# Second layer of the expert network: blocks 1 to 23 by seven block products instead of eight, interleaved with the groups of the first layer; ScalarE centers rows

## The reference

```python
top_w, top_i = jax.lax.top_k(rw_tok, K)            # K = 2 experts, the same for all tokens
top_w = jax.nn.softmax(top_w, axis=-1)
h = jax.nn.gelu(jnp.einsum('nd,edf->enf', xf, W1) + b1[:, None, :], approximate=False)   # 256 -> 512
y = jnp.einsum('enf,efd->end', h, W2) + b2[:, None, :]                                   # 512 -> 256
out = jnp.einsum('ne,end->nd', w_dense, y)
out = _layer_norm(out + x, gamma, beta)            # the expert network's own x is normalised
x = x + out
```

## Time and profile before

| | us |
|---|---|
| median of 3 runs | 804.6 |
| profiled execution | 804.91 |
| its span | 803.0 |
| TensorE busy in the span | 761.0 |
| VectorE, ScalarE, GpSimd busy | 567.7, 479.4, 414.3 |
| TensorE busy in 500.96 to 782.78 us | 281.82 |

### The profile page before, as it was taken

One profiled execution on the slowest core, in us unless ns is written; L12 is line 12 of the kernel. 1 busy time (PEld: TensorE's weight loads), 2 busy tenths in 40 slices (PEclk: granted clock), 3 DMA queues, 4 the chain that ended last, 5 costly groups with the idle time before them and its releaser, 6 DMA issues. The chain is left out here.

```text
span 803.0 us, 15427 instructions
## 1 busy us (share of the span) xinstructions
PE 761.0 (95%) x4960; PEld 622.9 (78%) x4960; DVE 567.7 (71%) x1623; ACT 479.4 (60%) x1113; POOL 414.3 (52%) x649
## 2 busy tenths in 40 slices
PE   6899999999899999999849999999999999999996
PEld 5678888888566666676526788888888888888885
DVE  6863488788678888888888755655666666566656
ACT  2467345989899988888728425444444444444440
POOL 3430778778458888888717712333333333333323
PEclk9999999999999999999959989999999999999999
DMA  8855122222112211212101040000000000000001
GB/s 217 208 158 161 39 58 51 59 52 53 26 32 63 59 51 35 62 25 65 42 22 38 20 130 3 27 13 26 14 27 16 24 25 16 26 14 26 16 25 38
DMA packets 35423, 41.33 MB, mean 51 GB/s; under 512 B 11520, under 2 KB 20696, under 8 KB 35339
## 3 DMA queue, kind: packets, MB, share of 16 engines
q1 hardware_dynamic: 22355, 30.71, 13.3%
q0 software_dynamic: 8000, 6.82, 3.9%
q10 hardware_dynamic: 4984, 2.79, 1.5%
HBM read 25.59 MB, written 14.60 MB: 50 GB/s over the span
## 5 line engine op out<-in xcount | busy, mean ns | idle before, releaser
L1379 PE MATMUL ps<-Z 128*125 128x256 f32 x800 | 195.5, 379 | 0.7 <-DVE L L1987 0.7
L1379 PEld LDWEIGHTS ps<-Z 128*125 128x125 f32 x800 | 149.6, 187 | 22.2 <-DVE L L1987 1.1
L1116 PE MATMUL ps<-Z,L 128*128 128x250 f32 x600 | 126.9, 373 | 0.0
L1116 PEld LDWEIGHTS ps<-Z,L 128*128 128x128 f32 x600 | 113.6, 189 | 13.2
L1007 ACT ACTIVATE Z<-Z,b1s 128x250 f32<-128x250 f32 x144 | 68.4, 503 | 78.6 <-DVE Z L1980 78.5
L1980 DVE TENSOR_TENSOR Z<-ps,L 128x250 f32<-128x250 f32 x144 | 60.1, 419 | 76.8 <-PE ps L1362 76.6
L700 POOL TENSOR_SCALAR zr<-zmv 125x1 f32<-125x1 f32 x50 | 11.5, 230 | 199.3 <-issue 189.4
L1014 ACT ACTIVATE L<-ps 128x250 f32<-128x250 f32 x144 | 54.4, 380 | 65.5 <-PE ps L1362 63.6
L1236 PE MATMUL ps<-wr,Z 128*125 128x256 f32 x400 | 92.7, 384 | 0.0
L1362 PE MATMUL ps<-L 128*128 128x250 f32 x288 | 84.0, 374 | 0.0
L852 ACT ACTIVATE Z<-Z,bn_o,bn_s 128x250 f32<-128x250 f32 x150 | 81.2, 599 | 1.0 <-DVE bn_o L1690 1.0
...
## 6 DMA issues: line engine op xcount, KB each, us to landing
...
```

Of the source, the lines that this page charges most:

```text
L1116: last = mm(ps[:, group_bank(n), h * BT:(h + 1) * BT], wq[:, k, c * 128:(c + 1) * 128], h_raw(b, k), start=(k == 0), stop=(k == KD - 1))
L1379: last = mm(ps[0:TP, R_BANK + t, 0:D], ge_of(b, f)[:, t * TP:(t + 1) * TP], w2s[:, f // NF, f % NF, :], start=(k == 0), stop=(k == TOP_K * ...
```

## The change

For blocks 1 to 23 the second layer is computed by seven block products as well (`result_times`): the 250 x 1024 by 1024 x 256 product of a block is cut in two token halves, two experts and two output halves (`HD2` = 128 columns). Each product is four matmuls of 128 x 125 stationary by 128 x 128 moving. Blocks 0 and 24 keep the plain form (`whole_result`). With it come:

- four sums of GELU outputs for each block on GpSimd (`sum_of_g`, tensors of 128 x 500), and four sums of `w2s` once on VectorE (`weight_sum`);
- seven reads of PSUM by VectorE for each block, 125 x 128 each (`take_part`), in place of two of 125 x 256;
- rows centered by ScalarE (`center`), so that `make_row` on VectorE is one instruction;
- both halves' scale in one pair of GpSimd instructions (`z_scale`);
- the first layer's two blocks of a pair change places (`blocks`), so that the block consumed first has its GELU outputs first;
- other places for the tensors, and PSUM banks shared between slots: 0 and 1 for the first layer's sums, 2 and 3, 6 and 7 for the second layer.

```diff
+            def sum_of_g(b, i):
+                if i == S_1:
+                    pool.wait_ge(gelu_done, gelu_of_block(b))
+                after = {S_1: P5, S_2: P6, S_4: P3, S_3: P7}[i]
+                if b >= 2:
+                    pool.wait_ge(y_part.sem, y_part.count(b - 2, after))
+                if i == S_1:
+                    g.tensor_tensor(gs[:, 0], ge_part(b, 0, 1), ge_part(b, 1, 1), ALU.add).then_inc(n.sem, 1)
...
-            for s in range(SLOTS + 5):
-                n = s - 3
-                if n >= 0:
-                    z_scale(n)
-                if 0 <= n + 1 < TB * NB:
-                    x_and_offset(n + 1)
-                if s + NF < SLOTS:
-                    sum_of_h(s // NF + 1, s % NF)
+            for b in range(-1, NB - 1):
+                if b >= 1:
+                    for i in (S_1, S_2, S_4):
+                        sum_of_g(b, i)
+                    z_scale(b - 1)
+                    sum_of_g(b, S_3)
+                if b >= 0:
+                    x_and_offset(b)
+                p, half = divmod(b + 3, 2)
+                if NF * p < SLOTS:
+                    for i in range(2 * half, 2 * half + 2):
+                        sum_of_h(p, i)
...
+            def center(b, t):
...
+                a_.activation(za(b, t)[0:TP], x_of(b, t), ACT.Identity, bias=negmu[0:TP, b, t:t + 1]).then_inc(centered, 1)
...
+            center(0, 1)
+            center(0, 0)
             for i, l in ((1, 2), (2, 2), (1, 1), (2, 1)):
...
+            def result_times(b, n):
+                of = {P1: ge_part(b, 0, 0), P5: gs[:, 0], P6: gs[:, 1], P3: gs[:, 3],
+                      P7: gs[:, 2], P2: ge_part(b, 1, 0), P4: ge_part(b, 1, 1)}[n]
...
+                if n == P7:
+                    pe.wait_ge(g_sums.sem, g_sums.count(b - 1, S_3))
+                    pe.wait_ge(y_sum.sem, y_sum.count(b - 1, KEPT_U))
...
+                for k in range(NF):
+                    last = mm(ps[0:TP, bank, 0:HD2], of[:, k], by[:, k], start=(first and k == 0),
+                              stop=(k == NF - 1), skip_group_check=True)
+                last.then_inc(y_part.sem, 1)
+
+            def whole_result(b, t, k0, k1):
+                for k in range(k0, k1):
+                    f = F_ORDER[k]
+                    if k == 0 and t == 0:
+                        if b:
+                            pe.wait_ge(y_sum.sem, y_sum.count(b - 2))
...
+            for b in range(1, NB - 2):
+                g = 2 * b + 2
+                times(g, P1)
+                times(g, P5)
+                result_times(b, P1)
...
+            for n in (P1, P5, P6, P3, P7, P2, P4):
+                result_times(NB - 2, n)
+            for t in range(TB):
+                whole_result(NB - 1, t, 0, 8)
...
+            def take_part(b, n):
+                x_, z_, y_ = (ps[0:TP, bank, 0:HD2] for bank in (XR_BANK[b % 2], ZR_BANK, YR_BANK))
+                after, to, part, other, needs = {
+                    KEPT_1: (P1, kz[0][0:TP], x_, za(b, 0)[0:TP, lo], None),
+                    KEPT_5: (P5, kz[1][0:TP], z_, za(b, 1)[0:TP, hi], None),
+                    KEPT_U: (P6, kz[2][0:TP], x_, za(b, 0)[0:TP, hi], None),
+                    Z_12: (P3, zz[0][0:TP, hi], z_, kz[2][0:TP], KEPT_U),
+                    Z_22: (P7, zz[1][0:TP, hi], x_, kz[1][0:TP], KEPT_5),
+                    Z_11: (P2, zz[0][0:TP, lo], y_, kz[0][0:TP], KEPT_1),
+                    Z_21: (P4, zz[1][0:TP, lo], x_, za(b, 1)[0:TP, lo], None)}[n]
...
+                v_.tensor_tensor(to, part, other, ALU.add).then_inc(y_sum.sem, 1)
...
+                take_part(b, Z_12)
+                make_y(b - 1, 0)
+                sum_of_products(g + 1, SUM_12)
+                make_row(b + 1, 0)
+                take_part(b, Z_22)
+                sum_of_products(g + 1, SUM_22)
+                make_y(b - 1, 1)
+                sum_of_products(g + 1, SUM_11)
+                take_part(b, Z_11)
...
+            b = NB - 2
+            take_part(b - 1, Z_21)
+            stats(b - 1, 0)
+            take_part(b, KEPT_1)
...
+            make_y(b - 1, 1)
+            stats(b, 0)
+            take_part(b, Z_21)
+            stats(b, 1)
```

More of the change, by code:

```diff
@@ L444, in gps_layer @@
         SUM_12, SUM_22, SUM_11 = 1, 2, 3
+        S_1, S_2, S_4, S_3 = 1, 2, 3, 4
+        Z_12, Z_22, Z_11, Z_21 = 4, 5, 6, 7
+        STATS, MOMENTS = (1, 2), (3, 4)
         F_ORDER = (0, 2, 1, 3, 4, 6, 5, 7)
@@ L1972, in sum_of_products @@
                 f1, f2 = NF * e + c, NF * e + c + 2
+                b1_, b2_ = blocks(p)
                 bank, after, k, to = {
-                    SUM_12: (Z_BANK[s], P3, KEPT_U, ge_of(2 + 2 * p, f1)),
-                    SUM_22: (X_BANK[s], P7, KEPT_5, ge_of(2 + 2 * p, f2)),
-                    SUM_11: (Y_BANK[s], P2, KEPT_1, ge_of(1 + 2 * p, f1)),
+                    SUM_12: (z_bank(g), P3, KEPT_U, ge_of(b2_, f1)),
+                    SUM_22: (X_BANK[s], P7, KEPT_5, ge_of(b2_, f2)),
+                    SUM_11: (y_bank(g), P2, KEPT_1, ge_of(b1_, f1)),
                 }[n]
@@ L2026, in make_y @@
                                         op0=ALU.mult, op1=ALU.add).then_inc(y_ready.sem, 1)
             dve.wait_ge(ln_in, 32)
[L2029 to L2042 removed]
+            make_row(0, 1)
@@ new lines, in _ @@
+            make_row(0, 0)
+            sum_of_products(2, SUM_12)
+            weight_sum(1)
+            sum_of_products(2, SUM_22)
+            sum_of_products(2, SUM_11)
+            weight_sum(2)
+            whole_z(0, 0)
+            make_row(1, 1)
+            sum_of_products(3, SUM_12)
+            weight_sum(3)
+            make_row(1, 0)
+            sum_of_products(3, SUM_22)
+            sum_of_products(3, SUM_11)
+            weight_sum(4)
+            whole_z(0, 1)
+            for b in range(1, NB - 2):
+                g = 2 * b + 2
+                if b >= 2:
+                    take_part(b - 1, Z_21)
+                stats(b - 1, 0)
+                stats(b - 1, 1)
+                take_part(b, KEPT_1)
+                moments(b - 1, 0)
+                moments(b - 1, 1)
+                sum_of_products(g, SUM_12)
+                center_z(b - 1, 0)
+                take_part(b, KEPT_5)
+                sum_of_products(g, SUM_22)
+                sum_of_products(g, SUM_11)
+                center_z(b - 1, 1)
+                take_part(b, KEPT_U)
+                make_row(b + 1, 1)
+                take_part(b, Z_12)
[7 more added lines that the diff above has]
+                take_part(b, Z_11)
@@ new lines, in _ @@
+            take_part(b, Z_11)
+            make_y(b - 1, 1)
+            stats(b, 0)
+            take_part(b, Z_21)
+            stats(b, 1)
+            moments(b, 0)
+            moments(b, 1)
+            center_z(b, 0)
+            center_z(b, 1)
+            make_y(b, 0)
+            make_y(b, 1)
+            b = NB - 1
+            for t in range(TB):
+                whole_z(b, t)
+                stats(b, t)
+                moments(b, t)
+                center_z(b, t)
+                make_y(b, t)
```

319 lines of the change are left out of this document (219 added, 100 removed).

## The result

The changed kernel takes 795.81 us, the median of 4 runs (792.75 to 797.12), against 805.31 us for the kernel before in the same comparison (804.39 to 806.46, 4 runs): ratio 0.9876 [0.9844, 0.9908]. Run again later it took 793.43 us (791.59 to 796.18, 5 runs), ratio 0.9866 [0.9844, 0.9887]. It is faster, by about 1.3%. The profiled execution is the one of 792.75 us, the fastest of the four, so its span shows more of a gain than the median does. Forecast were 793.0 us for the median, range 788 to 802.

A forecast was written before the change was run, and what follows sets the result against it. TensorE was taken to bound the mixed loop. Loop -13.9, tail +1.7, start +0.1 and shared cover +0.5 sum to -11.6 us from the profiled 804.91, so 793.3; the median lies 0.3 lower: 793.0 us, range 788 to 802.

The forecast's parts named there:

- The bound: Mixed loop: TensorE is busy for all of its 281.82 us and alone sets its length.
- The pace, 0.112: Second layer in the loop: 0.112 us per 128-column instruction, bounds 0.108 and 0.114; 13.9 us gained over 44 slots.
- VectorE, GpSimd, ScalarE: Loop: the other engines keep up; VectorE 8.7 and GpSimd 8.4 us of a 12.18 us block, tightest margin 0.63.
- R7: One second-layer product group on TensorE; forecast not to wait for GpSimd's sums in the loop, but 1.1 us in the tail.
- The shared cover, 0.5 us: Loop: VectorE row operations stand still beside GpSimd; 11 odd blocks at 0.05 us, bounds nothing and 9 us.
- P4': First-layer product in a block's second slot, needing VectorE's SUM_22'; margin forecast at 0.63 us, 0.18 with port waits.
- The start, 0.1: Before the loop: two center instructions ahead of the first GELUs delay slot 2's first product by 0.1 us.
- The tail, 1.7: After the loop: TensorE pauses 1.1 us before R7 and 1.3 before whole_result; 1.7 us lost in all.
- Partial stalls: Rival, loop: margin missed by some 0.3 us in most blocks, or pace 0.117; still faster, 799.5 us; chance 0.22.
- Slower by the pace: Rival, loop: weight loads not hidden behind 128 columns; break-even 0.1234 us, 809 us at 0.125; chance 0.07.
- Slower by the port pair: Rival, loop: each of six VectorE row operations waits for a long GpSimd sum; 834 us; chance 0.06.
- No change through waits at P4': Rival, loop: a block's 0.63 us gain goes again in waits at P4', 12 us; 804.6 us; chance 0.05.

The follow-up runs named there:

- e_moving64: Changed kernel with the second layer's moving side cut from 128 to 64 columns in blocks 1 to 23: 794.27 us, one execution.
- e_short_sums: Changed kernel with each of GpSimd's four sums per block on 16 elements instead of 500: 791.19 us, ratio 0.9826 to the kernel before.
- e_more_sums_2: Changed kernel with two extra GpSimd additions of 128 x 125 ahead of each of a block's four sums: 806.95 us, ratio 1.0035 to the kernel before.
- e_start: Changed kernel with GpSimd's x_and_offset of block 0 held until VectorE has made b2w: 792.73 us, ratio 0.9848 to the kernel before.
- e_rows_on_dve: Changed kernel with rows centered and scaled by VectorE again instead of centered by ScalarE: 808.13 us, ratio 1.0036 to the kernel before.

## Why the prediction was right, step by step

**The bound.** Right. TensorE bounded the loop and still does: 265.28 us busy of 265.93, for before.

**The pace, 0.112.** Right in kind, too high in size. It is 0.1095, so the loop without waits gains 281.82 - 264.75 = 17.1 us and not 13.9. The row chosen from the earlier trace rows had loads of 128 columns; here they have 125. Three columns of 128 would be just the difference (0.112 x 125 / 128 = 0.1095), and e_moving64 shows that these loads alone give 0.109, but no run changes them by three columns alone. The bound of 0.108 was the nearer one. The Trainium skill's page "TensorE: Matmul & The Clock Gate", section "Back-to-back issue gap", gives about 81 ns in a stream of loads and matmuls against 56 isolated, which the prediction carried over as 25 ns on each instruction. The loop shows 1.5 at most (0.1095 against 0.108).

**VectorE, GpSimd, ScalarE.** Right in the main. `take_part` 0.29 (0.277 to 0.292 measured), sums 1.15 (1.07 to 1.17 by line, 1.25 for L771 where it doesn't stand), `center` up to 0.50 (0.499), GpSimd 8.4 us a block (189.28 / 22 = 8.6), VectorE 8.7 before any wait at the port was too much: 189.40 / 22 = 8.6 counts the waits beside GpSimd's sums, and e_short_sums, without most of them, has 175.78 / 22 = 8.0. R7 never waited for S in the loop, and e_more_sums_2 shows that it does once GpSimd is full.

**The shared cover, 0.5 us.** The place was right; that the size fits is in part luck, since it lies between two cases that the text didn't tell apart. The clock let the second center_z, due at 5.01, run only once `x_and_offset` had ended at 5.63; with the 0.28 of the earlier trace rows that ends at 5.9, 0.89 in all, and L2230 takes 0.888. It had the tightest margin at P4', and the waits are there and nowhere else. But what decides is which of make_y(b - 1, 0) and S_1 runs first. Where it is make_y, 0.57 us are left before P4', not 0.18. Where it is S_1, 0.59 us are lost. The profiles show 0, 2 and 5 such blocks of 11, nothing to 3.0 us; the 0.5 lies within. The lock of the Trainium skill's page "SBUF — State Buffer", section "SBUF: two separate sides", agrees with the rows of 1.58 beside 1.25 and of 1.54 where make_y runs first.

**The start, 0.1.** Wrong in its place. The text looked at the GELUs behind `center`. What is late is `b2w`: GpSimd's first `x_and_offset` no longer waits for VectorE's row (3.62 us before) but for `center` (0.83), starts at 486.18 instead of 488.53, and the sums behind it stretch L2152 and L2154 from 0.34 and 0.48 to 0.72 and 0.82. It costs 0.7 us, and e_start gives them back. The text checked GpSimd against VectorE in the loop and not ahead of it. The other 0.5 of the later loop lie before these stages and vary from run to run.

**The tail, 1.7.** Right in both pauses and their causes; 2.4 by the profile. The pause before R7 is 1.06 (1.1 forecast), that before `whole_result` 1.62 (1.3). What was left out of the latter: the four `x_and_offset` of blocks 23 and 24 run back to back beside VectorE's rows, of which three take 0.94 to 1.03 instead of 0.48. VectorE and GpSimd there, the first of the three:

```profile
772.07 0.99 DVE L2161 SCALAR_TENSOR_TENSOR wr<-wr,rstd,L 125x256 f32<-125x256 f32 x1
772.74 3.14 POOL L760 TENSOR_TENSOR Z<-Z,L 125x256 f32<-125x256 f32 x4
```

Counted from start to start TensorE is 1.26 us late at R7 and 1.79 at `whole_result`, more than the brackets say, since these begin at the modelled end of the matmul before.

**The sum.** -11.6 forecast, -12.3 in the span of the fastest execution, -9.5 between the medians of the first comparison (795.81, 2.8 above the forecast of 793.0), 793.43 in the second. It isn't as exact as it looks: the loop gained 2.5 more than forecast (15.9 against 13.9 - 0.5), start and tail lost 1.8 more (1.2 + 2.4 against 0.1 + 1.7). That these errors nearly cancel is luck.

**The rivals.** Partial stalls: the pace is below 0.112 and not at 0.117, and P4' waits in at most 5 of the 22 blocks, not in most. Slower by the pace: the break-even of 0.1234 was never near. Slower by the port pair: the lock is as strong as it supposed, 1.1 us for one operation behind a long sum, but one or two of the six in a block meet one at the wrong time, and the margins take it. e_rows_on_dve is that rival come true with one instruction more. No change through waits at P4': the right place, which in the changed kernel costs 0.59 us in some odd blocks, and in e_rows_on_dve (282.43 - 264.75) / 11 = 1.6 in all eleven.
